# Moving the per-chunk products of a delta-rule layer out of its recurrence, into items of one tile

## Chip, cores and metric
One core of a Trainium2 chip. The metric is the device time of one execution in microseconds (us); "before" is the median of three runs. Shorter is better.

## What is computed
Token ids (8 x 512) pick rows of an 8000 x 256 table; an attention layer of 16 heads of 16 channels (a delta rule with a running average, in chunks) is added to them, then a feed-forward layer with a router (top 2 of 8 experts and one shared expert, 256 -> 512 -> 256). All is float32. The kernel uses chunks of 32 tokens, 16 per batch. The heart of the reference, for one chunk i with keys K, queries Q, values V and B = beta * K:

```
T = tril(B @ K.T, -1);  inv = inverse(eye + T)
U = inv @ (V - B @ W_t)
W_new = W_t + K.T @ U
O = Q @ W_avg * a + Q @ W_t * c + T_mat * (Q @ K.T) @ U
W_avg_new = coef1 * W_avg + coef2 * W_t + K.T @ (U * w)
```

With Y = inv B and Z = inv V the update is U = Z - Y W, so that Y and Z need no state. Only W and W_avg go from chunk to chunk.

## The kernel before
It has three blocks that follow one another, each with one program per engine, in an order written out by hand; the engines meet at semaphores.

**First stage**, a loop over the 8 batches (512 tokens, 4 tiles of 128). GpSimd gathers the rows (`embed`), VectorE normalises them, TensorE turns them (`turn_x`, L378) and projects them to k, q, v in six 512-column groups (`project`, L399), the betas between the second and third (`beta`, L387). ScalarE copies each projection out twice (L490, L493), VectorE adds the three convolution taps (L577). Norms of k and q follow (`norms`, `spread_norms`, L408, L426, VectorE L609 to L625), the masks on ScalarE (L516, L521), and the Gram matrices and scores in two halves (`gram`, L452), taken by VectorE as ng (L642) and sT (L647). SP stores k, beta k and v, ng, scores and q to DRAM and loads the Gram matrices back, one chunk and pair of heads per partition (nx). The inverse is solved on VectorE by 62 half steps per batch (`half_step`, L172 and L175, both inputs in SBUF), dealt out between the other VectorE operations of the next two batches. Batches 0 to 5 are solved here, with the first 44 half steps of batch 6.
GpSimd also gathers the residual stream h in lane order (32 gathers) and adds the output bias to its 32 tiles (L366) while batches 0 to 2 run.

**Second stage**, the recurrence: 32 steps, two groups of 16. A step takes one chunk of four batches ("lanes"). TensorE applies the inverse to beta k and v (`yz`, 16 matmuls, L811, against a block-diagonal inverse), ScalarE copies that out twice (L938, L939), TensorE picks Z (`take_z`, 16 matmuls, L821), adds Y times the state (`read_y`, L833), ScalarE copies u (L945). Then `grow` (L859) sums K^T U, VectorE masks the new state (L1025), `read_q` (L847) reads the state by the queries, scaled on GpSimd (L789, four at a time), and `inside` adds scores times U (64 matmuls, L870). The output is normalised per head, turned, projected (`project`, L887), added to h (L1052), normalised and routed. VectorE does the rest of the inverses of batches 6 and 7 in steps 0 to 9, eight half steps per step. SP loads the inputs of step s+2 when the buffers of step s are free, in one queue.

**Third stage**: the shared expert on all batches, then 71 slots of 128 rows through the experts; TensorE is in it from 904 us on (L1229, L1235, L1264, L1271, L1286).

A matmul of float32 appears as two records in the profile, a transpose as one.

## Time and profile before

| what | value |
|---|---|
| runs, us | 1505.49, 1498.99, 1519.77; median 1505.49 |
| profiled execution, us | 1498.91, span 1497.1 |
| granted clock of TensorE, mean | 0.849 of full |
| busy: TensorE, VectorE, ScalarE, GpSimd | 1164.3, 749.3, 452.9, 321.9 us |

Engines in the rows: PE is TensorE, PEld its weight loads, DVE VectorE, ACT ScalarE, POOL GpSimd, SP the queue that issues DMAs. A row of a timeline has start, duration, engine, line, operation, output and inputs, and in brackets how long the engine was idle before it and what released it. "issue" means that the profile shows nothing that it waited for. In rows of busy times the order of engines is PE, PEld, DVE, ACT, POOL, each with its number of instructions.

### The profile page before, as it was taken

The page shows a single profiled execution, that of the slowest core. Times are in us where ns is not written, and L with a number is a line of the kernel's source. Part 1 is how long each engine was busy: PE and PEld are TensorE (multiplying, and loading weights), DVE is VectorE, ACT ScalarE, POOL GpSimd, SP SyncE. Part 2 cuts the span into 40 slices and gives each one's busy share as a digit, 9 for nine tenths or more (in the row PEclk, how much of TensorE's full clock was granted, in tenths as well). Part 3 has the DMA queues.
Part 4 walks back from the last instruction along what each step waited for, and adds up shares of the span by engine and source line. Part 5 has one row for each costly group of instructions (what it writes and reads, how often), then busy time and mean ns, then how long its engine had stood idle before and what let it go on. Part 6 is the DMA issues. An engine that isn't in the chain of part 4 may idle for free. (4 is left out here: it accounts for less than half of the span.)

```text
span 1497.1 us, 35306 instructions
## 1 busy us (share of the span) xinstructions
PE 1164.3 (78%) x14558; PEld 796.8 (53%) x14558; DVE 749.3 (50%) x1707; ACT 452.9 (30%) x889; POOL 321.9 (22%) x309
## 2 busy tenths in 40 slices
PE   4843765665655067778887878999999999999997
PEld 2632434434444056666676764665566666666664
DVE  4689999899999436754444453112111121211111
ACT  3540534424435022222332323331122222222221
POOL 3686101000000011110011104661022222222222
PEclk9875777778778557687888878999999999999999
DMA  7642555464556676567665619952132222223222
GB/s 272 189 145 63 147 153 116 132 162 103 143 111 158 160 158 152 130 143 165 157 148 141 160 56 342 346 167 78 28 47 47 46 47 44 46 47 47 47 46 29
DMA packets 232444, 184.00 MB, mean 123 GB/s; under 512 B 148165, under 2 KB 196197, under 8 KB 227937
## 3 DMA queue, kind: packets, MB, share of 16 engines
q1 hardware_dynamic: 198000, 149.20, 38.0%
q0 software_dynamic: 16368, 19.96, 7.6%
q10 hardware_dynamic: 17920, 12.59, 3.1%
q8 instruction: 119, 1.95, 0.5%
q14 instruction: 37, 0.30, 0.1%
HBM read 101.69 MB, written 86.26 MB: 126 GB/s over the span
## 5 line engine op out<-in xcount | busy, mean ns | idle before, releaser
L1420 DVE TENSOR_TENSOR hid_all<-p_s,silu 128x512 f32<-128x512 f32 x103 | 71.3, 692 | 378.5 <-PE p_s L1271 249.7
L1470 POOL DMA_INDIRECT out_h<-y_sb,x_in x71 | 110.8, 1560 | 360.7 <-DVE y_sb L1432 342.8
L1328 ACT ACTIVATE silu<-p_m 128x512 f32<-128x512 f32 x103 | 61.5, 597 | 328.2 <-PE p_m L1264 223.4
L175 DVE TENSOR_TENSOR xt<-xt,prod 128x62 f32<-128x62 f32 (+15 forms) x248 | 151.8, 612 | 4.3
L1286 PE MATMUL p_y<-wo,hid_all 128*128 x568 | 134.4, 380 | 0.8 <-ACT hid_all L1345 0.8
L1264 PE MATMUL p_m<-wi,xT_c 128*128 x284 | 133.6, 593 | 0.5 <-ACT xT_c L1341 0.5
L1271 PE MATMUL p_s<-ws,xT_c 128*128 x284 | 133.6, 593 | 0.0
L172 DVE TENSOR_TENSOR prod<-nx,xt 128x62 f32<-128x62 f32 (+15 forms) x248 | 129.6, 523 | 2.6
L577 DVE SCALAR_TENSOR_TENSOR cv<-raw,conv_sb,cv 128x512 f32<-128x512 f32 x144 | 107.0, 747 | 18.0 <-ACT raw L493 17.2
L1286 PEld LDWEIGHTS p_y<-wo,hid_all 128*128 128x128 f32 x568 | 102.5, 190 | 12.3 <-issue 1.4
L452 PE MATMUL p_g<-kqM,kT 32*32 32x128 f32 x2048 | 50.7, 369 | 71.2 <-DVE sT L647 53.8
L399 PE MATMUL p_p<-xT,wqkv_sb 128*128 128x512 f32 x192 | 105.2, 706 | 0.7 <-ACT xT L487 0.7
L490 ACT ACTIVATE cv<-p_p,now_b,conv_sb 128x512 f32<-128x512 f32 x48 | 37.3, 777 | 198.8 <-PE p_p L399 198.8
L789 POOL TENSOR_TENSOR qq<-qq,cst_early 128x512 f32<-128x512 f32 x32 | 33.8, 1089 | 286.4 <-DMA qq<-q_channels_dram 286.4
L452 PEld LDWEIGHTS p_g<-kqM,kT 32*32 32x32 f32 x2048 | 43.3, 133 | 76.7 <-issue 74.0
L870 PE MATMUL p_o<-u,sT_b 32*32 32x16 f32 x4096 | 52.6, 191 | 37.7 <-issue 37.6
L811 PE MATMUL p_yz<-xbd,bv_b 128*32 128x128 f32 x1024 | 43.2, 316 | 43.6 <-DMA xbd<-chunk_inverse_dram 34.5
L1264 PEld LDWEIGHTS p_m<-wi,xT_c 128*128 128x128 f32 x284 | 53.9, 190 | 38.3 <-issue 34.7
L1432 DVE COPY y_sb<-p_y 128x256 f32<-128x256 f32 x71 | 30.2, 425 | 85.5 <-PE p_y L1286 85.5
L1460 POOL DMA_INDIRECT slots_in_dram<-rows,slot_of x64 | 62.1, 971 | 45.8 <-ACT rows L1336 32.3
L870 PEld LDWEIGHTS p_o<-u,sT_b 32*32 32x32 f32 x4096 | 47.0, 121 | 45.5 <-issue 45.3
L399 PEld LDWEIGHTS p_p<-xT,wqkv_sb 128*128 128x128 f32 x192 | 42.0, 232 | 53.8 <-issue 45.3
(139 smaller groups left out, 1938.0 us busy)
## 6 DMA issues: line engine op xcount, KB each, us to landing
slots_in_dram<-h SPq DMA_DIRECT2D x9, 1040.0 KB, 10.0
x_in<-slots_in_dram SPq DMA_DIRECT2D x71, 130.0 KB, 2.1
k_tokens_dram<-kk SPq DMA_DIRECT2D x32, 256.0 KB
chunk_gram_dram<-ng SPq DMA_DIRECT2D x32, 256.0 KB
beta_kv_dram<-bv SPq DMA_DIRECT2D x32, 256.0 KB
nx<-chunk_gram_dram SPq DMA_DIRECT2D x8, 1024.0 KB, 4.9
xt<-in_const SPq DMA_DIRECT2D x8, 1024.0 KB, 8.0
scores_dram<-sT SPq DMA_DIRECT2D x32, 256.0 KB
```

The source lines that it names most:

```text
L172: ins = dve.tensor_tensor(pr, nx[b % 2][:, m, :, 0:m].rearrange("p e k -> p k e").unsqueeze(3).to_broadcast([P, m, 2, w]), xt[b % 2][:, m, ...
L175: ins = dve.tensor_tensor(kept, kept, pr, ALU.add)
L399: ins = pe.matmul(p_p[n % 2][:], wqkv_sb[:, k, p, m * P:(m + 1) * P], xT[:, k, :], start=(k == 0), stop=(k == KH - 1))
L452: ins = pe.matmul(p_g[c * C:(c + 1) * C, g % 4, t % 2, g // 4, :], kT[r, g // 4, tok], kqM[r, g // 4, :, :, tok].rearrange("p w e i -> p ( ...
L577: ins = dve.scalar_tensor_tensor(cv[:, p, m, :], raw[:, p, m, j:j + L], conv_sb[:, p, m, j:j + 1], cv[:, p, m, :], ALU.mult, ALU.add)
L870: ins = pe.matmul(p_o[lane(b), hd * DH:(hd + 1) * DH], sT[s % 2][lane(b), hd, :], u[s % 2][lane(b), hd * DH:(hd + 1) * DH], start=(chunk(s ...
L1264: ins = pe.matmul(p_m[n % 2][:], xT[s % 2][:, k, :], wi[:, e, k, :], start=(k == 0), stop=(k == KH - 1))
L1271: ins = pe.matmul(p_s[n % 2][:], xT[s % 2][:, k, :], ws[:, e, k, :], start=(k == 0), stop=(k == KH - 1))
L1286: ins = pe.matmul(p_y[s % 2][:, 0, :], hidT[s % 2][:, f * P:(f + 1) * P], wo[:, e, f, :], start=(f == 0), stop=(f == FK - 1))
L1420: dve.tensor_tensor(dst, p_s[n % 2][:], silu[n % 2][:], ALU.mult).then_inc(S["hid_ready"], 1)
L1460: pool.indirect_dma_start(xs_dram, bass.IndirectOffsetOnAxis(slot_of[:, t, k:k + 1], 0), rows[q][:, k, :], None).then_inc(s_scat[q], 16)
L1470: pool.indirect_dma_start(token_rows, bass.IndirectOffsetOnAxis(x_in[s % X_IN][:, D:D + 1].bitcast(U32), 0), y_sb[s % 2][:], None, compute ...
```

## The change
The work of a chunk that needs no state leaves the steps. It is done in "items": one item is one tile (four chunks) of one batch, 32 in all. An item loads inverse, beta k and v, and scores in one transfer (`load_item`), and its queries twice; applies the inverse (`apply_inverse`, 64 matmuls) giving -Y and Z; turns Y (`turn_y`); applies the scores to both (`apply_scores`, 64 matmuls), giving the part of the output that needs no state and a correction of the queries; adds the correction to the scaled queries (`sum_queries`, one matmul of 512 columns and four of 128); and stores all three (`store_item`). GpSimd scales the queries of an item (`scale_item`). A step then adds Z and the inner output by one matmul each (`take_z`, `take_o`), and Y and the corrected queries read the state as before; `yz`, `inside` and their copies are gone.

Items 0 to 19 (batches 0 to 4) are made in the first stage, four per batch from batch 3 on; items 20 to 31 (batches 5 to 7) in steps 0 to 3, 5 to 8 and 12 to 15 of the second stage. The two transposing banks of PSUM of the first stage become the items' banks, and x and v are turned in the projections' banks. In the first stage kk, bv, ng and sT now lie in the space of h, so the lane gather and the bias of h move to GpSimd in the second stage, and the slots' zero block is half as large. SP's order, ScalarE's order and VectorE's order in a step change with it. The stores of the scores and of beta k and v are one and two transfers instead of four and four. The third stage is unchanged.

```diff
+        AHEAD = 3
+        ITEMS = B * TILES
+        IN_A = TILES * (B - AHEAD)
+        R = 3
+        item = [sb(tail, f"item{i}", [P, 3, H, C]) for i in range(R)]
...
+        def load_item(sp, r):
+            b, t, i = r // TILES, r % TILES, r % R
+            if r >= R:
+                sp.wait_ge(T["q_summed"], r - R + 1)
+            sp.wait_ge(s_xst, 16 * HP * (b + 1))
+            sp.wait_ge(s_st, STORES * (b + 1))
+            sp.dma_start(item[i][:].rearrange("p w h i -> p (w h i)"),
+                         solve_dram[b, t * P:(t + 1) * P].rearrange("p w x -> p (w x)")).then_inc(s_item[i], 16)
...
+        def store_item(sp, r):
+            b, t, i = r // TILES, r % TILES, r % 2
+            at = (b // GROUP, slice(t * CH, (t + 1) * CH), slice(None), b % GROUP)
+            sp.wait_ge(T["y_ready"], r + 1)
+            sp.dma_start(y_dram[at].rearrange("c p x -> p c x"), y_out[i][:].rearrange("p c n i -> p c (n i)")
+                         ).then_inc(s_y_st[i], 16)
+            sp.wait_ge(T["yz_ready"], r + 1)
+            sp.wait_ge(T["inner_ready"], r + 1)
+            for c in range(CH):
+                sp.dma_start(zo_dram[t * CH + c, b], yzo[i][tok(c), 1:3].rearrange("p w h d -> p (w h d)")
+                             ).then_inc(s_zo_st[i], 16)
+            sp.wait_ge(T["q_ready"], r + 1)
+            sp.dma_start(qy_dram[at].rearrange("c p x -> p c x"), qy_out[i][:].rearrange("p c n i -> p c (n i)")
...
+        def scale_item(pool, r):
+            t, i = r % TILES, r % R
+            pool.wait_ge(s_item_q[i], 32 * (r // R + 1))
+            pool.tensor_tensor(item_q[i][:], item_q[i][:],
+                               table("q_scale")[:, t * P:(t + 1) * P].unsqueeze(1).to_broadcast([P, HQ, P]),
+                               ALU.mult).then_inc(T["q_scaled"], 1)
...
+        def apply_inverse(pe, r, bank, alone):
+            i = r % R
+            pe.wait_ge(s_item[i], 16 * (r // R + 1))
+            if r:
+                pe.wait_ge(T["fix_ready"], r)
+                pe.wait_ge(T["inner_ready"], r)
+                if alone:
+                    pe.wait_ge(T["q_ready"], r)
+            bv_i = item[i][:, 1].rearrange("p h i -> p (h i)").rearrange("p (w h d) -> p w h d", w=2, d=DH)
+            for hd in range(H):
+                for c in range(CH):
+                    ins = pe.matmul(bank[tok(c), hd * C:(hd + 1) * C], item[i][tok(c), 0, hd, :], bv_i[tok(c), :, hd, :],
+                                    start=True, stop=True)
+            ins.then_inc(T["solved"], 1)
...
+        def turn_y(pe, r, bank, alone):
+            pe.wait_ge(T["yz_ready"], r + 1)
+            if r and not alone:
+                pe.wait_ge(T["q_ready"], r)
+            for n in range(HQ):
+                ins = pe.transpose(bank[0:4 * DH, n * P:(n + 1) * P],
+                                   yzo[r % 2][:, 0, 4 * n:4 * n + 4, :].rearrange("p h d -> p (h d)"), ident)
+            ins.then_inc(T["y_turned"], 1)
...
+        def apply_scores(pe, r, bank, alone):
+            i = r % R
...
+            for hd in range(H):
+                for c in range(CH):
+                    ins = pe.matmul(bank[tok(c), hd * C:(hd + 1) * C], item[i][tok(c), 2, hd, :], yzo[r % 2][tok(c), 0:2, hd, :],
+                                    start=True, stop=True)
+            ins.then_inc(T["scored"], 1)
...
+        def sum_queries(pe, r, bank, alone):
+            pe.wait_ge(T["y_ready"], r + 1)
+            pe.wait_ge(T["fix_ready"], r + 1)
...
+            pe.wait_ge(T["q_scaled"], r + 1)
+            pe.matmul(bank[:], ident, item_q[r % R][:].rearrange("p n l -> p (n l)"), start=True, stop=False, skip_group_check=True)
+            for n in range(HQ):
+                ins = pe.matmul(bank[0:4 * DH, n * P:(n + 1) * P], q_fix[r % 2][:, n, :], ident, start=False, stop=True,
+                                skip_group_check=True)
+            ins.then_inc(T["q_summed"], 1)
...
+        def yz_out(act, r, bank):
+            act.wait_ge(T["solved"], r + 1)
...
+                        i0 = TILES * (b - AHEAD)
+                        if b >= AHEAD:
+                            load_item(sp, i0 + 2)
+                            if i0:
+                                store_item(sp, i0 - 1)
+                            load_item(sp, i0 + 3)
+                            store_item(sp, i0)
...
+                        if b >= AHEAD:
+                            store_item(sp, i0 + 1)
+                        if b + 1 >= AHEAD:
+                            load_item(sp, i0 + TILES)
...
+                                if b >= AHEAD:
+                                    store_item(sp, i0 + 2)
+                                if b + 1 >= AHEAD:
+                                    load_item(sp, i0 + TILES + 1)
...
-                    for s in range(NT):
-                        if s == NT // 2:
-                            embed(RING + 1)
-                        pool.tensor_tensor(h[:, s, :], h[:, s, :], bout_sb[:], ALU.add)
...
+                    for b in range(AHEAD, B):
+                        if b + 2 < B:
+                            embed(b + 2)
+                        for t in range(TILES):
+                            scale_item(pool, TILES * (b - AHEAD) + t)
...
                     for b in range(B):
                         pe.wait_ge(s_xT, b * KH + KH)
                         project(b, 0)
                         project(b, 1)
+                        solve_item(b, 0)
+                        score_item(b, 0)
                         beta(b)
-                        for n in range(2, 6):
-                            project(b, n)
+                        project(b, 2)
+                        project(b, 3)
+                        end_item(b, 0)
+                        solve_item(b, 1)
+                        project(b, 4)
+                        project(b, 5)
                         norms(b)
                         turn_v(b)
+                        score_item(b, 1)
                         spread_norms(b)
                         turn_k(b)
+                        end_item(b, 1)
+                        solve_item(b, 2)
+                        score_item(b, 2)
                         gram(b, 0)
+                        end_item(b, 2)
+                        solve_item(b, 3)
                         if b + 1 < B:
                             turn_x(b + 1)
+                        score_item(b, 3)
                         gram(b, 1)
+                        end_item(b, 3)
...
+                        scored_item(b - 1, 3)
+                        ended_item(b - 1, 3)
...
+                            if n == 1:
+                                solved_item(b, 0)
+                                scored_item(b, 0)
+                            if n == 3:
+                                ended_item(b, 0)
+                                solved_item(b, 1)
...
+                        scored_item(b, 1)
...
+                        ended_item(b, 1)
+                        solved_item(b, 2)
...
+                        scored_item(b, 2)
+                        ended_item(b, 2)
+                        solved_item(b, 3)
...
+            step_of = {IN_A + k: k for k in range(4)}
+            step_of |= {IN_A + 4 + k: 5 + k for k in range(4)}
+            step_of |= {IN_A + 8 + k: 12 + k for k in range(4)}
+            item_in = {s: r for r, s in step_of.items()}
...
+                    def load_step(s):
...
                         if s >= 2:
...
+                        if c % CH == 0:
+                            sp.wait_ge(s_y_st[t % 2], 16 * done)
+                            sp.wait_ge(s_zo_st[t % 2], 16 * CH * done)
+                            sp.wait_ge(s_qy_st[t % 2], 16 * done)
+                        if c:
+                            sp.dma_start(yy[i][:].rearrange("p b n i -> p (b n i)"), y_dram[g, c].rearrange("p b x -> p (b x)")
...
+                        sp.dma_start(zo[i][:].rearrange("p w d -> p (w d)"),
+                                     zo_dram[c, b:b + GROUP].rearrange("b i x -> (b i) x")).then_inc(s_zo[i], 16)
...
                     for s in range(NT):
-                        if s == 6:
+                        load_step(s)
+                        if s == 3:
                             store_inverse(sp, B - 2)
-                        if s == 14:
+                        if s == 11:
                             store_inverse(sp, B - 1)
-                        if s == NC_BATCH:
...
+                        if s - 2 in item_in:
+                            store_item(sp, item_in[s - 2])
+                        if s + 1 in item_in and item_in[s + 1] >= IN_A + 2:
+                            load_item(sp, item_in[s + 1])
...
+                    pool.wait_ge(s_weights, 16 * 5)
...
+                    def add_bias(n):
+                        pool.wait_ge(s_lane[n % 4], 16 * (n // 4 + 1))
+                        pool.tensor_tensor(h[:, n, :], h[:, n, :], bout_sb[:], ALU.add).then_inc(s_hb, 1)
...
+                    scale_item(pool, IN_A)
+                    scale_item(pool, IN_A + 1)
+                    pool.memset(h[:, 4:], 0.0).then_inc(s_hz, 1)
+                    pool.wait_ge(s_hz, 2)
+                    for n in range(NT):
+                        add_bias(n)
+                        if n + 4 < NT:
+                            gather(n + 4)
+                        if n + 1 in item_in and item_in[n + 1] >= IN_A + 2:
+                            scale_item(pool, item_in[n + 1])
 
                 @block.tensor
...
+                        ins = pe.matmul(p_u, ident, zo[s % 2][:, 0], start=True, stop=(chunk(s) == 0), skip_group_check=True)
...
+                        ins = pe.matmul(p_o[:], ident, zo[s % 2][:, 1], start=True, stop=(chunk(s) == 0), skip_group_check=True)
...
                     for s in range(NT + 4):
+                        r = item_in.get(s)
+                        if s < NT:
+                            read_y(s)
                         if s >= 4:
                             route(s - 4)
+                        if r is not None:
+                            apply_inverse(pe, r, p_i, True)
                         if s < NT:
-                            read_y(s)
+                            grow(s)
+                            take_o(s)
                             read_q(s)
+                        if r is not None:
+                            turn_y(pe, r, p_i, True)
                         if 1 <= s <= NT:
                             turn_o(s - 1)
-                        if s < NT:
-                            grow(s)
-                            if s + 1 < NT:
-                                yz(s + 1)
-                            inside(s)
+                        if 2 <= s < NT + 2:
+                            turn_xn(s - 2)
+                        if r is not None:
+                            apply_scores(pe, r, p_i, True)
                         if 1 <= s <= NT:
                             project(s - 1)
                         if s + 1 < NT:
                             take_z(s + 1)
-                        if 2 <= s < NT + 2:
-                            turn_xn(s - 2)
+                        if r is not None:
+                            sum_queries(pe, r, p_i, True)
...
                     for s in range(NT + 2):
+                        r = item_in.get(s)
                         if s < NT:
                             u_out(s)
+                        if s >= 2:
+                            row_sqrt(s - 2)
+                        if r is not None:
+                            yz_out(act, r, p_i)
+                        if s < NT:
+                            square(s)
+                        if r is not None:
+                            turned_y_out(act, r, p_i)
                         if 1 <= s <= NT:
                             oT_out(s - 1)
-                        if s + 1 < NT:
-                            yz_out(s + 1)
+                        if s >= 2:
+                            xnT_out(s - 2)
+                        if r is not None:
+                            scored_out(act, r, p_i)
                         if s < NT:
-                            square(s)
                             head_sqrt(s)
-                        if 1 <= s <= NT:
-                            row_sqrt(s - 1)
+                        if r is not None:
+                            queries_out(act, r, p_i)
...
                     for s in range(NT + 4):
+                        if 2 <= s < NT + 2:
+                            norm(s - 2)
+                        solve(SHARE * s)
+                        if s >= 4:
+                            take_score(s - 4)
+                        if s < NT:
+                            state_out(s)
+                        solve(SHARE * s + 2)
+                        if s < NT:
+                            head_sum(s)
                         if s >= 4:
                             gate(s - 4)
-                        solve(SHARE * s)
-                        if s < NT:
-                            state_out(s)
-                            head_sum(s)
-                        solve(SHARE * s + 2)
-                        if 1 <= s <= NT:
-                            residual(s - 1)
                         solve(SHARE * s + 4)
                         if s < NT:
                             head_norm(s)
                         solve(SHARE * s + 6)
                         if 1 <= s <= NT:
-                            norm(s - 1)
+                            residual(s - 1)
```

## Rows read from the trace of the kernel before

**Rows 1.** Busy times by stretch; columns: stretch, length, busy us, clock, DMA share, GB/s.
```profile
63.00:124.00 61.00, 33.56 (x426) 24.37 (x417) 54.43 (x79) 24.46 (x40) 50.13 (x55) 0.75 0.53 141
...
249.00:309.00 60.00, 35.33 (x384) 25.15 (x384) 55.25 (x115) 24.58 (x40) 0.00 (x0) 0.76 0.53 133
...
689.00:879.00 190.00, 158.14 (x5350) 130.02 (x5342) 88.66 (x330) 59.23 (x146) 16.92 (x16) 0.82 0.63 146
...
904.00:1497.00 593.00, 581.94 (x2074) 354.32 (x2074) 113.93 (x197) 148.87 (x310) 179.69 (x167) 0.99 0.36 88
```
**Rows 2.** Timeline (start us, us, engine, line, operation): projections 2 to 5 of batches 1, 2, 6, 7.
```profile
68.84 7.11 PE L399 MATMUL p_p<-xT,wqkv_sb 128*128 128x512 f32 x16
...
149.66 9.99 PE L399 MATMUL p_p<-xT,wqkv_sb 128*128 128x512 f32 x16
...
389.45 9.56 PE L399 MATMUL p_p<-xT,wqkv_sb 128*128 128x512 f32 x16
...
449.21 8.70 PE L399 MATMUL p_p<-xT,wqkv_sb 128*128 128x512 f32 x16
```
**Rows 3.** Timeline: betas of batches 0 and 6; Gram halves after batch 6's projections.
```profile
26.35 1.86 PE L387 MATMUL p_g<-wbeta_sb,xT 128*128 128x16 f32 x16
...
386.04 3.57 PE L387 MATMUL p_g<-wbeta_sb,xT 128*128 128x16 f32 x16 [8.42 <-DVE sT L647]
...
420.31 2.20 PE L452 MATMUL p_g<-kqM,kT 32*32 32x128 f32 x128 [1.83 <-ACT kqM L521]
...
425.88 0.68 DVE L642 TENSOR_TENSOR ng<-p_g,neta 128x512 f32<-128x512 f32 x1
...
430.22 3.53 PE L452 MATMUL p_g<-kqM,kT 32*32 32x128 f32 x128 [6.69 <-DVE sT L647]
```
**Rows 4.** Timeline of batch 1: a half step and the bias adds.
```profile
103.60 11.74 DVE L175 TENSOR_TENSOR xt<-xt,prod 128x462 f32<-128x462 f32 x1
103.93 10.91 POOL L366 TENSOR_TENSOR h<-h,bout_sb 128x256 f32<-128x256 f32 x16
```
**Rows 5.** Timeline of ScalarE: u of steps 1, 15, 16 and 31.
```profile
543.62 0.37 ACT L945 COPY u<-p_u 128x256 f32<-128x256 f32 x1 [0.54 <-PE p_u L833]
...
713.23 0.37 ACT L945 COPY u<-p_u 128x256 f32<-128x256 f32 x1 [0.28 <-PE p_u L833]
...
720.97 0.37 ACT L945 COPY u<-p_u 128x256 f32<-128x256 f32 x1 [0.28 <-ACT xnT L983]
...
878.91 0.37 ACT L945 COPY u<-p_u 128x256 f32<-128x256 f32 x1 [1.30 <-PE p_u L833]
```
**Rows 6.** Timeline of TensorE: the second part of one score group.
```profile
707.57 1.07 PE L870 MATMUL p_o<-u,sT_b 32*32 32x16 f32 x101 [2.98 <-issue]
```
**Rows 7.** The page's third part, DMA queues: packets, MB, share.
```profile
q8 instruction: 119, 1.95, 0.5%
```
**Rows 8.** Timeline: GpSimd's multiplies and VectorE operations beside them.
```profile
563.12 4.23 POOL L789 TENSOR_TENSOR qq<-qq,cst_early 128x512 f32<-128x512 f32 x4 [24.45 <-DMA qq<-q_channels_dram]
...
566.56 0.88 DVE L172 TENSOR_TENSOR prod<-nx,xt 128x62 f32<-128x62 f32 x1
...
707.74 4.23 POOL L789 TENSOR_TENSOR qq<-qq,cst_early 128x512 f32<-128x512 f32 x4 [42.78 <-DMA qq<-q_channels_dram]
...
710.68 0.42 DVE L1052 TENSOR_TENSOR h<-p_turn,h 128x256 f32<-128x256 f32 x1 [1.17 <-PE p_turn L887]
```
**Rows 9.** Timeline of TensorE: groups at the upper clock, first and second stage.
```profile
422.44 1.09 PE L378 MATMUL p_t<-cst,xhat 128*128 128x128 f32 x8
...
713.88 1.08 PE L811 MATMUL p_yz<-xbd,bv_b 128*32 128x128 f32 x32
...
715.89 1.18 PE L870 MATMUL p_o<-u,sT_b 32*32 32x16 f32 x118 [0.70 <-issue]
...
719.27 0.64 PE L821 MATMUL p_u<-cst_early,yz_ch 128*32 128x64 f32 x27 [0.91 <-issue]
```
**Rows 10.** Chain that ended last, last stage: start us, us, engine, tile, line.
```profile
934.67 1.72 PE p_m L1229 x4
```

389 lines of the change are left out of this document (198 added, 191 removed).

## Prediction

> **What bounds the kernel now.** I read the busy times by stretch first, then the timeline of each engine around the seams. The kernel has three stages. The last, from 904 us on, is TensorE at 98% busy under a full clock [rows 1]; no line of the change touches it, so its 593 us stand [rows 1]. All that can move lies in the first 904 us.
> In the first stage one batch takes 59.8 us (389.45 to 449.21) [rows 2], and VectorE is the bound: in a batch-long window it is busy 55.25 of 60 us, while TensorE has 35.33, ScalarE 24.58, at a mean granted clock of 0.76 [rows 1]. TensorE waits for VectorE twice per batch, 8.42 us before the betas and 6.69 us before the second half of the Gram matrices [rows 3]. One batch is longer: from 68.84 to 149.66 is 80.8 us [rows 2]. There a half step of the inverse, normally 0.6 us, stands in VectorE for 11.74 us, exactly while GpSimd adds the output bias to 16 tiles of h in 10.91 us [rows 4]; the same pair comes once more at 121 us.
> In the second stage (recurrence, 32 steps) TensorE is the bound: 158.14 of 190 us busy at a clock of 0.82 [rows 1]. From step 1 to step 31 the copies of u stand 335.3 us apart, 11.2 us a step; the best step is 7.74 us (713.23 to 720.97) [rows 5]. The difference between 7.7 and 10.5 (the mean after step 13) has two sources. One is the clock. The other is holes in the middle of the score group, 2.98 us in the row, released by nothing the profile shows [rows 6]; they come about once per step, and the instruction queue fetches 119 blocks over the whole span [rows 7].
>
> **Part 1: bias and lane gather leave the first stage.** The two VectorE stalls go: 11.74 and 11.75 less the 0.65 that such a step takes, -22 us, of which I take -21.5 (80.8 against 59.3 for the batches around it). Nothing else was waiting in that batch that would take its place: TensorE there waited for the same VectorE results. In the second stage the bias adds (32 of them, 0.68 us each) and the gathers sit on GpSimd again; VectorE has two-SBUF-input work there only in the half steps of steps 0 to 9, so they cost at most some 5 us of VectorE time, inside steps that TensorE bounds. I take 0, bounds 0 to +6. Why PSUM matters: the residual add h<-p_turn,h ran in 0.42 us, its normal time, in the middle of a GpSimd run of four multiplies [rows 8].
>
> **Part 2: the query scaling joins the first stage.** 20 of the 32 items are scaled there by GpSimd, in one 128x512 multiply each; four of them took 4.23 us, 1.06 each [rows 8]. A half step that met such a run was held until its end (0.88 instead of 0.22 us) [rows 8]. Four items per batch, VectorE nearly all on such half steps and taps: up to 4 x 1.06 = 4.2 us per batch; an item whose multiply meets a PSUM operation or an idle moment costs nothing. I take 3.0, bounds 1 and 4.2.
>
> **Part 3: item work on TensorE and ScalarE in the first stage.** An item is two groups of 64 32x32 matmuls, 4 transposes, one 512-column matmul and four of 128 columns. At full clock: a score group of 118 records took 1.18 us, so 128 take 1.28; 8 transposes took 1.09, so 4 take 0.55; four records of 512 columns took 1.72, so two take 0.86, and four of 128 columns the same again [rows 9, 10]. Sum 2 x 1.28 + 0.55 + 0.86 + 0.86 = 4.8 us. At the low clock the betas took 3.57 instead of 1.86 [rows 3]; the item is then 8 to 9 us. Four items add 19 to 35 us to TensorE's 35 in a 60 us batch. ScalarE gets five copies per item, some 2.5 us, 10 per batch on 24.6: it has room.
> What decides is the place. Items 0 and 3 stand in the two waits of 8.42 and 6.69 us. There they are covered, and they keep TensorE busy through what is now idle time after which the clock is low. The end of item 0 and the solve of item 1 stand between projections 3 and 4, and the projections feed VectorE's taps with about 1 us to spare; at full clock they add 3.0 us, against which the betas give back up to 1.7 and the projections 2.4 (16 records took 9.56 us) if the clock has stayed up [rows 2, 3]. Then comes the scoring of item 1 before the norms are spread, covered by statistics and reciprocal on VectorE. Last, the end of item 1 and item 2 up to its scores stand before Gram half 0, whose second mask on ScalarE now also waits behind the copies of items 1 and 2: that group ended at 422.5, VectorE takes it at 425.88 [rows 3], 3.4 us of cover against some 4 to 6 us. The later half has 8 us of cover. I take +1.2 us per batch net for all of this, bounds 0 and +6. The added loads and stores (nine DMAs per item on SP's queue, some 18 us of issue per batch beside 20 now, and about 0.3 to 0.4 of DMA share beside 0.53 [rows 1]) stand in SP's queue before the stores of k and the load of the Gram matrices; that load has some 15 us before VectorE wants it. I take 0 and keep +4 per batch in the slow rival.
> First stage: -21.5 + 5 x (3.0 + 1.2) = -0.5 us; bounds -21.5 + 5 x 1 = -16 and -21.5 + 5 x 14 = +49.
>
> **Part 4: the recurrence.** Each step loses the Y/Z group (1.08), the scores group (1.28) and the picking of Z (27 records 0.64, so 32 take 0.76): 3.1 us at full clock. It gains two one-matmul additions of 256 columns, 0.43 each [rows 9, 10]. The best step of 7.7 becomes 5.5. A chain shows up under it: square, head sum, gate, root, normalisation, residual on VectorE and ScalarE, which I add up to 6.2 us from their own durations. The real mean is now 1.36 times the best (10.5 over 7.74) [rows 5]; with the same factor a plain step is 7.5, an item step (5.5 + 4.8) x 1.36 = 14.0 us. VectorE has 6 us of its own per step and 4.4 of half steps in steps 0 to 9, so the two plain steps there stay at the 11.2 of now. One more wait: the load of item 28 stands on SP behind the store of the last inverse (8 DMAs, 7.1 us of issue, then the landing), and the loads of step 12 stand behind it, so step 11 takes 13. Steps 1 to 30: 11 x 14.0 + 2 x 11.2 + 7.5 + 13 + 15 x 7.5 = 309.4 against 335.3 [rows 5]: -26. Bounds: item steps 11.5 to 12.5, plain 6.6: about -60; item steps at the low clock 16.5, plain 9: +30.
> Where the trace shows holes inside a group of matmuls, the Trainium skill (Runtime: NRT & Kernel Launch, Instruction fetch mechanics) says that instructions come in blocks of 256 by the sequencer's own DMA queue and that crossing a block costs mostly nothing. The 2.98 us row disagrees. By that page the holes would be nothing here and the item steps would be some 1.5 us cheaper, which would add about 18 us to the gain; the rows decide for me.
> The entry of the stage loses the wide loads (block-diagonal inverse, queries) and GpSimd's zeroing of xbd: -2. The exit gets one step more of latency (the normalisation of step 31 is one pass later): +1.
>
> **Sum.** The profiled execution took 1498.9 us (span 1497.1). -0.5 - 26 - 2 + 1 = -27.5 gives 1471. The median of the runs is 1505.5, 0.44% above, so 1478.
>
> **Rivals.**
> A. *Item work in the first stage is hidden and the low-clock stretches go.* GpSimd's multiplies mostly meet nothing (5 us in all), TensorE stays at the upper level, item steps near 12 and plain steps near 6.6. For: waits of 8.42 and 6.69 us, rows at both clock levels. Against: the half step held to the end. -16 - 55 - 1 = -72 at the far end, some -62: 1444.
> B. *TensorE becomes the bound of the first stage (slower).* Item groups are almost only tiny matmuls, the kind that shows the holes; with low clock and two blocks per item an item costs 8.6 + 1.5 = 10 us, four of them 40 on 35, with 4 us of serial waits (norms, roots) 79 us for a batch of 60. It decides from 64 us on, where it eats the 21.5 gained. Price: 5 x 19 = +95, less 21.5, less 27: +46, so 1552. For: a mean clock of 0.76. Against: the busier TensorE is, the higher the clock in these rows (0.99 in the last stage) [rows 1].
> C. *The recurrence gains nothing.* The 12 item steps take back what the plain steps give (16 us each against 7.5): 0 from that stage, first stage about 0: 1503 to 1510.
>
> **Chances.** Forecast (1455 to 1495) 0.45, A 0.22, C 0.19, B 0.14. Two per cent, which is about what a measurement of this kernel tells from no change (the three runs span 1.4%), is 30 us; the faster line is 1475.4, just below my number. Faster: A 0.22, and 0.21 of the forecast. Same: 0.24 of the forecast, 0.16 of C. Slower: B 0.14 and 0.03 of C. Range: from within A to within B, 1438 to 1530; the forecast's own range is 1455 to 1495.
>
> **What would show it.** Right: the 11.7 us half steps gone, batch 1 near 60 us; batches 3 to 7 at 63 to 66 us with half steps of 1 to 1.6 us beside GpSimd multiplies; TensorE's waits at the betas and the second Gram half shrunk to 0 to 3; plain steps 7 to 8 us, steps 12 to 15 near 14; a late step 11 or 12. Wrong: batches over 70 us with VectorE waiting for raw or p_g (B), plain steps still near 10 (then the chain on VectorE or the loads bound them), or the stretch from 904 on of another length.

## The result, and the profile after

The kernel after the change takes 1521.85 us (median of 20 runs, 1514.06 to 1530.2) against 1506.13 before (20 runs, 1497.45 to 1519.77): 1.0106 times as long, 95% interval 1.0083 to 1.0129. It is slower by 1.1%, clear of the noise of 20 runs each but inside the 2% that the prediction counts as no change; 1478 was forecast. The two profiled executions differ by more, since the one of before was near its fastest run: spans 1522.6 and 1497.1, +25.5 us. The rest of this section splits those 25.5.

Busy times by stretch after the change (stretch, length, busy us per engine, clock, DMA share, GB/s), against [rows 1]:
```profile
334.00:406.00 72.00, 54.51 (x1468) 38.72 (x1467) 58.77 (x114) 33.09 (x60) 5.54 (x4) 0.90 0.64 192
740.00:900.00 160.00, 139.10 (x3154) 105.62 (x3154) 94.07 (x352) 45.31 (x137) 34.97 (x40) 0.90 0.64 192
930.00:1522.60 592.60, 581.58 (x2074) 353.65 (x2073) 112.88 (x194) 148.91 (x310) 179.45 (x167) 0.99 0.36 87
```
The last stage is what it was. In a batch with items VectorE is busy 58.8 us, 3.5 more than before, but idle 13.2 of 72 (before 4.8 of 60), and TensorE, busy 54.5 at a clock of 0.90, isn't full either. So each waits in turn for a result of the other.

Timeline of TensorE: projections after the betas, batches 1, 2, 6, 7, against [rows 2] (there 68.84, 149.66, 389.45, 449.21):
```profile
67.73 7.11 PE L531 MATMUL p_p<-xT,wqkv_sb 128*128 128x512 f32 x16
...
125.03 5.24 PE L531 MATMUL p_p<-xT,wqkv_sb 128*128 128x512 f32 x6
...
406.06 5.38 PE L531 MATMUL p_p<-xT,wqkv_sb 128*128 128x512 f32 x8
...
484.25 5.68 PE L531 MATMUL p_p<-xT,wqkv_sb 128*128 128x512 f32 x8
```
Batch 1 has shrunk from 80.8 to 57.3 us, batch 6 has grown from 59.8 to 78.2. Starts of the betas give the sum: those of batch 3 come at 182.13 instead of 205.38 (-23.3), and from there to the first u it is 388.6 us instead of 322.9 (+65.7, 13.1 per batch). The first u stands at 570.76 instead of 528.28: +42.5.

Timeline of batch 6, ScalarE, VectorE and TensorE (in brackets: idle before, and what ended it):
```profile
421.09 0.59 ACT L294 COPY yzo<-p_item 128x512 f32<-128x512 f32 x1 [7.16 <-DMA z_and_inner_dram<-yzo]
...
422.96 0.75 DVE L769 SCALAR_TENSOR_TENSOR cv<-raw,conv_sb,cv 128x512 f32<-128x512 f32 x1 [5.87 <-ACT raw L671]
...
426.39 4.24 PE L540 MATMUL p_g<-kqM,cst_early 128*32 128x128 f32 x32 [8.24 <-ACT kqM L683]
...
446.81 2.01 PE L585 MATMUL p_g<-kqM,kT 32*32 32x128 f32 x107
452.08 1.10 PE L585 MATMUL p_g<-kqM,kT 32*32 32x128 f32 x21 [3.26 <-issue]
...
453.31 0.69 DVE L838 TENSOR_TENSOR h<-p_g,neta 128x512 f32<-128x512 f32 x1 [4.90 <-PE p_g L585]
```
Two things are to be seen. ScalarE's copy of Y and Z waits 7.16 us for a store of the item two before; the copies of projections 4 and 5 stand behind it, so VectorE waits for raw and TensorE 8.24 us for the squares. And the first Gram half, which stands behind the item groups, stops for 3.26 us in its middle with no releaser; VectorE then waits 4.90 us. Such a stop inside a group of matmuls, with nothing that the profile shows as waited for ("issue"), is called a hole below. The waits from 185 to 560 us, by line:
```profile
DVE cv L769 <- ACT raw L671: 35.0, 12, 5.9
...
PE p_g L585 <- issue: 21.6, 10, 3.3
DVE h L838 <- PE p_g L585: 20.8, 5, 5.5
PE p_item L273 <- issue: 20.2, 13, 3.6
ACT yzo L294 <- DMA z_and_inner_dram<-yzo: 19.6, 4, 7.2
```
(us in total, times, longest.) The holes of TensorE in this stretch, those of L253 included, add up to some 45 us, 9 per batch; before there are none from the betas of batch 3 on. The instruction queue fetches 140 blocks, of 16 KB each, instead of 119 [rows 7]:
```profile
q8 instruction: 140, 2.29, 0.6%
```
Recurrence: u of steps 1, 12, 13, 30 and 31 on ScalarE, against [rows 5], and the score group in the middle of step 2:
```profile
590.76 0.37 ACT L1123 COPY u<-p_u_turn_x 128x256 f32<-128x256 f32 x1 [0.45 <-PE p_u_turn_x L1019]
...
755.48 0.37 ACT L1123 COPY u<-p_u_turn_x 128x256 f32<-128x256 f32 x1 [9.35 <-PE p_u_turn_x L1019]
773.03 0.37 ACT L1123 COPY u<-p_u_turn_x 128x256 f32<-128x256 f32 x1 [0.45 <-PE p_u_turn_x L1019]
...
899.65 0.37 ACT L1123 COPY u<-p_u_turn_x 128x256 f32<-128x256 f32 x1 [1.78 <-PE p_u_turn_x L1019]
905.46 0.37 ACT L1123 COPY u<-p_u_turn_x 128x256 f32<-128x256 f32 x1 [1.78 <-PE p_u_turn_x L1019]
```
```profile
619.34 0.53 PE L273 MATMUL p_item<-yzo,item 32*32 32x32 f32 x20 [3.07 <-issue]
```
A plain step is 5.8 us, an item step mostly 17 to 20 (step 5 24.3, step 15 10.2), and in steps 1 and 2 the score group stops for 3.07 us at the same place, after 107 and 108 records. From step 0 to 31 it is 334.7 us instead of 350.6 (-15.9; from step 1, 314.7 instead of 335.3). From u of step 31 to the end: 617.1 instead of 618.2. +42.5 - 15.9 - 1.1 = 25.5.

What the holes wait for is in the same trace, in the packets of the instruction queue. From 20 to 910 us TensorE has 45 holes of over 0.5 us; 44 of them end 1.2 to 1.6 us after a packet of that queue has landed (before: all 29 of such holes). Each step with an item sees three such packets, only step 15 two; each plain step sees one, step 19 none.

### The profile page after: what moved, and what is told of

It is laid out like the page before. It is cut to its first block and busy times, and to the rows that moved or that the text cites. A ratio compares the mean times of both kernels' runs of the same rounds, so it can differ in the third digit from the quotient of the medians.

```text
span 1522.6 us, 40964 instructions
## 1 busy us (share of the span) xinstructions
PE 1246.2 (82%) x17182; PEld 836.7 (55%) x17182; DVE 742.0 (49%) x1707; ACT 478.9 (31%) x985; POOL 324.2 (21%) x308
## 5 line engine op out<-in xcount | busy, mean ns | idle before, releaser
L238 POOL TENSOR_TENSOR item_q<-item_q,cst_early 128x512 f32<-128x512 f32 x32 | 40.8, 1276 | 513.7 <-DMA item_q<-q_channels_dram 513.7
L769 DVE SCALAR_TENSOR_TENSOR cv<-raw,conv_sb,cv 128x512 f32<-128x512 f32 x144 | 115.9, 809 | 47.0 <-ACT raw L671 46.1
L174 DVE TENSOR_TENSOR xt<-xt,prod 128x62 f32<-128x62 f32 (+15 forms) x248 | 133.1, 536 | 4.4
L273 PE MATMUL p_item<-yzo,item 32*32 32x32 f32 x4096 | 51.2, 198 | 59.8 <-issue 55.6
L585 PE MATMUL p_g<-kqM,kT 32*32 32x128 f32 x2048 | 48.1, 327 | 42.7 <-issue 21.6
L273 PEld LDWEIGHTS p_item<-yzo,item 32*32 32x32 f32 x4096 | 44.2, 109 | 66.6 <-issue 66.1
L1652 POOL DMA_INDIRECT slots_in_dram<-rows,slot_of x64 | 62.1, 971 | 46.4 <-ACT rows L1528 33.1
L1624 DVE COPY y_sb<-p_y 128x256 f32<-128x256 f32 x71 | 30.1, 424 | 85.5 <-PE p_y L1478 85.5
L1463 PEld LDWEIGHTS p_s<-ws,xT_c 128*128 128x128 f32 x284 | 48.5, 191 | 34.4 <-issue 34.4
L1421 PE MATMUL p_m<-xnT_c,wi 128*128 128x512 f32 x128 | 62.0, 608 | 5.3 <-DMA wo<-in_w_out 5.3
```

The source lines that it names most:

```text
L174: ins = dve.tensor_tensor(kept, kept, pr, ALU.add)
L273: ins = pe.matmul(bank[tok(c), hd * C:(hd + 1) * C], item[i][tok(c), 2, hd, :], yzo[r % 2][tok(c), 0:2, hd, :], start=True, stop=True)
L769: ins = dve.scalar_tensor_tensor(cv[:, p, m, :], raw[:, p, m, j:j + L], conv_sb[:, p, m, j:j + 1], cv[:, p, m, :], ALU.mult, ALU.add)
L1421: ins = pe.matmul(p_m[n % 2][:], wi[:, SHARED, k, cols], xnT[b % 2][:, k, :], start=(k == 0), stop=(k == KH - 1))
L1463: ins = pe.matmul(p_s[n % 2][:], xT[s % 2][:, k, :], ws[:, e, k, :], start=(k == 0), stop=(k == KH - 1))
L1652: pool.indirect_dma_start(xs_dram, bass.IndirectOffsetOnAxis(slot_of[:, t, k:k + 1], 0), rows[q][:, k, :], None).then_inc(s_scat[q], 16)
```

## The experiments

Times are medians; a ratio is to the kernel before, run on the same chip in the same rounds. "First stage" is the time of the first u, "recurrence" the time from u of step 0 to u of step 31, both in the profiled execution. After the change they were 570.8 and 334.7.

**1. GpSimd's scaling left out of the first stage.**
```diff
-                        for t in range(TILES):
-                            scale_item(pool, TILES * (b - AHEAD) + t)
```


> Leaves out GpSimd's scaling of the queries of items 0 to 19 (20 multiplies of 1.09 us beside VectorE, so the rows of these queries are unscaled); all else as after the change. Theory lock (my prediction's part 2): VectorE, which bounds a batch, loses 3 us per batch to these multiplies, so five batches get 15 us shorter (5 to 21) and VectorE's busy time in batches 3 to 7 falls from about 58 to 55 us. Theory order (the batches are long because TensorE and ScalarE, which run their orders as written, bring projections, copies and Gram groups late): VectorE's busy time falls the same way, but its waits grow by as much; the total changes by 0 to -5 us and a batch stays at 72 to 77 us.


1517.85 us, 1.0079 [1.0048, 1.0110], 2 to 6 us less than after. VectorE's busy time from the betas of batch 3 to the first u falls from 291.3 to 279.2 us, 2.4 per batch, but its waits grow: for the betas from 7.2 to 11.7 us, for the norms from 1.3 to 7.5. Theory order holds: the time that the multiplies cost is real in VectorE's busy time, and worth about 1 us of a batch at the end.

**2. One matmul in place of each group of 64, first stage.** Values of Y, Z and scores product of items 0 to 19 aren't the real ones.
```diff
+            if not alone:
+                ins = pe.matmul(bank[:], ident, item[i][:, 0]..., start=True, stop=True)
-            for hd in range(H):
+            for hd in range(H if alone else 0):
```


> In the items of the first stage (0 to 19) the two groups of 64 matmuls of 32x32 are replaced by one 512-column matmul each, so Y, Z and the scores product of these items are not the real ones; waits, copies, DMAs and the places in the orders stay. Theory size (the groups cost TensorE what they last: 2 x 1.3 to 2.6 us plus the holes of 1 to 3.6 us seen in them, and what follows waits for it): some 5 to 8 us per batch go, total -25 to -40 us, TensorE's busy time per batch falls from 57 to about 47 us, and waits named issue in the middle of groups nearly vanish from the first stage. Theory order (each item is a chain of five hand-overs between TensorE and ScalarE standing in front of what VectorE wants, whatever the matmuls last): -5 to -15 us. Theory transfers (a batch is long because item transfers and their place in SP's queue hold ScalarE): 0 to -5.


1465.72 us, 0.9744 [0.9693, 0.9796], 56 less than after: more than any theory gave. Only 23 us of it lie in the first stage (548.0). The recurrence, whose own groups are untouched, went from 334.7 to 296.9. The stage part supports size. The rest raised the question of runs 5 and 6: the edit takes 20 x 126 matmuls of four instructions out ahead of the recurrence, 10080, which is 39 blocks of 256 and 96 more, so the blocks of the recurrence end elsewhere as well (100 blocks are fetched instead of 140).

**3. A third buffer for Y, Z and inner outputs.**
```diff
-yzo = [... for i in range(2)]
+yzo = [... for i in range(3)]
...
-            if r >= 2:
-                act.wait_ge(s_zo_st[r % 2], 16 * CH * (r // 2))
+            if r >= 3:
+                act.wait_ge(s_zo_st[r % 3], 16 * CH * (r // 3))
```


> Three buffers for Y, Z and the inner outputs instead of two, so ScalarE's copy of Y and Z no longer waits for the store of the item two before. Theory transfers: the waits of 6.3, 3.6, 7.2 and 2.6 us in batches 4 to 7 go, and since five projections' worth of taps stand behind them, -15 to -20 us in total (a batch of 71 to 72 instead of 75). Theory order or size: VectorE finds its next late result within the same batch (the Gram group, the norms), so at most -8 us.


1510.96 us, 1.0039 [1.0009, 1.0069], 11 less than after. The wait for the store is gone from ScalarE's list, VectorE's for raw falls from 35.0 to 23.0 us. First stage 558.9 in this profile (569.9 in run 15, whose first stage is the same code: single profiles differ by this much, 570.8 and 574.6 for the changed kernel itself). The total, not this difference, is what shows the gain: the two ratios to before, 1.0039 and 1.0106, have intervals that don't meet. It lies between the two theories (15 to 20, at most 8). A cause, but the smaller one.

**4. The scoring of item 2 behind the first Gram half.**
```diff
-                        score_item(b, 2)
                         gram(b, 0)
+                        score_item(b, 2)
```


> On TensorE the scoring of item 2 stands behind the first half of the Gram group instead of in front of it. Theory order: VectorE's wait for the first Gram half (3.0 to 5.5 us per batch, 20.8 us in all) goes, and TensorE's scoring falls into the time between the halves, where TensorE waits for VectorE: -10 to -20 us. Theory size or transfers: the group comes earlier but the later steps (end of item 2, solve of item 3, transposes of x, second half) come later by as much: 0 to -5 us.


1526.06 us, 1.0129 [1.0078, 1.0179]: nothing gained. VectorE's waits for Gram halves are 24.3 us, now ten times instead of five, and the first half waits for ScalarE's masks of q, which stand behind the item copies (16.2 us in five).

**5. Moved block ends.** Extra tiny matmuls at the start of TensorE's program.
```diff
+                    for _ in range(16):      # 32 and 48 in the other two
+                        pe.matmul(p_i[0][0:32, 0:32], ident[0:32, 0:32], ident[0:32, 0:32], start=True, stop=True)
                     turn_x(0)
```


> 16 extra 32x32 matmuls (64 instructions: each is two weight loads and two matmuls) at the very start of TensorE's program, before anything waits for it; all else as after the change. They shift where the blocks of the fetched instruction stream end. Theory fetch: the holes named issue stand where a block ends inside a dense run of tiny matmuls, and an item step of the recurrence is 772 instructions by my count, close to 3 x 256, so the holes stand at the same place in each item step; with another shift they fall elsewhere: steps 0 to 31 of the recurrence, 334.7 us, change by more than 8 us in at least one of the three shifts (297 to 345), and the first stage (571 us) by more than 5 us. Theory data: the recurrence of the run with one matmul per group was short (297 us) because its data were other ones; then all three shifts give 333 to 338 us there and 568 to 573 us before it.

> As the run before, with 32 extra matmuls (128 instructions). Theory fetch: half a block away from where the change stands now, the hole of 3.07 us leaves the middle of the score group; recurrence 300 to 325 us. Theory data: 333 to 338 us.

> As the run before, with 48 extra matmuls (192 instructions). Theory fetch: different from the other two shifts and from none by more than 8 us in the recurrence. Theory data: 333 to 338 us.


1533.89, 1534.95 and 1527.16 us, ratios 0.9891, 0.9894 and 0.9857, on a chip where the kernel before took 1549.7; the changed kernel wasn't run on it, so the ratios say nothing of the shift. Recurrences: 328.6, 331.5 and 307.0 us. The holes in them add up to 40, 42 and 30 us, against 50 in the changed kernel. First stages: 591.9, 587.9 and 600.6 us, which can't be told from what made before slow there. The third shift speaks for theory fetch, whose figure for half a block (300 to 325) failed; with no unshifted run beside them the three don't show it, runs 11 and 15 do.

**6. The same shift in the kernel before.**


> The kernel before the change with 32 extra 32x32 matmuls at the start of TensorE's program. Its steps are not a multiple of 256 instructions, so its 20 holes at L870 already fall at every place: theory fetch gives 1500 to 1512 us (within 0.5% of before), with the long and the short steps of the recurrence in other places of the list. If instead its time moves by more than 1%, the comparison of the two kernels itself hangs on where the blocks end.


1552.5 against 1549.7 us, 1.0011 [0.9981, 1.0041]: no difference, as the ratio was expected; the 1500 to 1512 us were not met, because this chip took 1549.7 without the shift too.

**7. The changed kernel again**, on a chip like the first.


> The changed kernel itself, on the same chip as the next three, because the chip of the shift runs ran the kernel before at 1550 us instead of 1505. Ratio to before 0.985 to 1.012, whichever chip it is; on a chip like the first, recurrence 333 to 338 us, first stage 568 to 575.


1522.79 us, 1.0123 [1.0075, 1.0172]; first stage 574.6, recurrence 333.4.

**8. Item steps spread over the recurrence.**
```diff
+            step_of = {IN_A + k: s for k, s in enumerate((0, 1, 3, 4, 6, 7, 9, 10, 13, 17, 21, 25))}
...
+                        if 1 <= s < 3:
+                            pe.wait_ge(S["h_ready"], s)
```


> The 12 item steps of the recurrence are spread: steps 0, 1, 3, 4, 6, 7, 9, 10, 13, 17, 21, 25 instead of 0 to 3, 5 to 8, 12 to 15 (one wait is added in steps 1 and 2 to keep a bank free of collisions). Same instructions otherwise. Theory fetch: three blocks per item step cannot be fetched in the step, but a plain step uses less than one, so a plain step between lets the queue catch up: item steps of 12 to 14 us instead of 17 to 18, plain ones 5.8 to 7, recurrence 275 to 310 us. Theory chain (an item step is long because the hand-overs of an item between TensorE and ScalarE stand in line with those of the step): 17 us wherever the item stands, recurrence 330 to 338.


1535.76 us, 1.0234 [1.0187, 1.0280]; recurrence 337.4, in a profile that is the fastest of the four runs (1521.72), so the median's 13 us over run 7 aren't in it. Item steps still take 16.5 to 23.7 us early on and 13.7 to 15.5 late, with longer neighbours (8.2, 9.4 and 7.6 us before the last three). The late ones are shorter than the 17 of theory chain, but the recurrence as a whole is no shorter: a plain step between does not let the queue catch up, and that part of theory fetch is refuted.

**9. Runs 2 and 3 together.**


> Both at once: three buffers for Y, Z and inner outputs, and one 512-column matmul in place of each group of 64 in the items of the first stage (their values are not the real ones). Alone they gave 12 and 23 us of the first stage, while with one matmul the waits for the store grew from 19.6 to 37.8 us. Theory: size and transfers are the two causes and nothing else of weight is left, so a batch is 60 to 64 us and the first stage 520 to 535 us long (as long as before, 528). Rival: the hand-overs in front of the projections and the Gram group cost by themselves, a batch stays above 66 us, first stage over 545.


1441.01 us, 0.9582 [0.9539, 0.9625]. First stage 515.7; batches 3 to 6 by the betas' starts 62.1, 62.2, 63.5, 59.7 us:
```profile
244.00:307.00 63.00, 49.64 (x459) 31.60 (x460) 59.69 (x117) 33.11 (x60) 10.33 (x9) 0.89 0.81 240
```
VectorE is nearly full again. The two causes together are 55 us of the first stage, alone 23 and some 10: with short groups the store wait had grown from 19.6 to 37.8 us, with a third buffer the groups still were late. Of the 65.7 us that the stretch from the betas of batch 3 to the first u had gained, 10.4 are left (333.3 against 322.9, 2.1 per batch), with the same transfers (DMA share 0.81), the same copies and the same places.

**10. Dense run, one place of the array.** 512 matmuls of 32x32 at two starts.


> Two runs of 512 extra 32x32 matmuls (2048 instructions, 8 blocks of 256), one at the start of TensorE's program, one at the start of its part of the recurrence; nothing else uses TensorE there. At the 20 ns per matmul of the trace they last 10.2 us each (20 at the low clock). Theory fetch: such a run is bound by the fetching of blocks, with a hole of 2.5 to 3.5 us about every 64 matmuls: 30 to 40 us each. Theory that blocks are read ahead and cost nothing: 10 to 21 us each, and the holes in the item groups have another cause.


One run, 1616.08 us. Timeline of TensorE, the two runs of 512:
```profile
11.43 54.82 PE L607 MATMUL p_item<-cst 32*32 32x32 f32 x1024 [11.43 <-DMA bbeta_sb<-in_bbeta]
...
609.09 54.82 PE L1092 MATMUL p_item<-cst 32*32 32x32 f32 x1024 [21.06 <-DMA ids_lane_sb<-in_ids_lane]
```
54.82 us at a granted clock of 1.00 and 54.82 at 0.50, 107 ns each, without one hole. Here every matmul uses the same place of the array, and 64 of them last 6.9 us, so the run doesn't test what dense groups like the items' do. It does show that blocks can come without a hole when each lasts 6.9 us: 8 instruction packets were fetched during the first run. Its recurrence took 332.1 us, though 512 matmuls, eight whole blocks, stand ahead of it twice.

**11. Third buffer and 192 instructions at the start.**


> Third buffer for Y, Z and inner outputs and the 192 instructions of shift, together, full computation. If where the blocks end is what made that run's recurrence 307 us on the slow chip: 12 us from the buffer and some 20 to 28 from the recurrence, 1480 to 1492 us. If the shift's gain was chance of that one profile: 1508 to 1514 us.


1487.62 us, 0.9886 [0.9838, 0.9934]; first stage 571.0, recurrence 302.4. Before took 1501.51 us here, and the record numbers the chip as that of runs 5 and 6.

**12. Dense run as the items have it**, four row groups in turn.
```diff
+                    for k in range(512):
+                        pe.matmul(p_i[tok(k % 4), k // 4 % 16 * 32:...], ident[tok(k % 4), 0:32], ident[tok(k % 4), 32:64], start=True, stop=True)
```


> As the dense run, but consecutive matmuls use the four row groups of the array and sixteen places of the bank in turn, like the item groups. Theory fetch: 20 ns each inside a block, and a hole of 3 to 5 us after each 64, so 4.5 to 6 us per block and 36 to 48 us per run of 512. Theory that the holes belong to the hand-overs of the item (semaphores, operands) and not to the instruction stream: no holes, 10 to 20 us per run.


One run, 1578.78 us. Timeline of TensorE in the first of the two:
```profile
11.45 3.68 PE L607 MATMUL p_item<-cst 32*32 32x32 f32 x223 [11.45 <-DMA bbeta_sb<-in_bbeta]
15.77 2.14 PE L607 MATMUL p_item<-cst 32*32 32x32 f32 x128 [0.64 <-issue]
19.50 1.99 PE L607 MATMUL p_item<-cst 32*32 32x32 f32 x128 [1.59 <-issue]
23.79 2.17 PE L607 MATMUL p_item<-cst 32*32 32x32 f32 x128 [2.29 <-issue]
27.80 1.93 PE L607 MATMUL p_item<-cst 32*32 32x32 f32 x128 [1.84 <-issue]
32.91 1.93 PE L607 MATMUL p_item<-cst 32*32 32x32 f32 x128 [3.18 <-issue]
```
After the first 223 records a hole after every 128, that is 64 matmuls or 256 instructions, with no operand to wait for and nothing else on the engine: 3.7 to 5.4 us from block to block here, 3.5 to 5.1 in the second run, 32.6 and 30.1 us per 512 instead of 10.2 at 20 ns each (36 to 48 were expected by theory fetch). The 1024 added matmuls add 16 blocks to the 140, so a block is 64 of them:
```profile
q8 instruction: 156, 2.56, 0.7%
```
The queue's packets in the trace close the argument. In the first of the two each hole ends 1.2 to 1.6 us after one has landed (those that end at 19.50, 23.79 and 27.80 us after landings at 17.91, 22.42 and 26.63), and a packet takes 0.9 to 1.2 us. From 15.77 us on it starts only 1.0 to 3.2 us after the block before it has begun to run; these three times make up the 3.7 to 5.4 us. The holes belong to the instruction stream. The clock doesn't enter: between the holes a block runs in 1.93 to 2.17 us at a granted 1.00 and in 1.93 to 2.20 us at 0.50. The recurrence took 333.4 us behind its eight whole blocks.

**13. One matmul per group in the recurrence's items** (values of items 20 to 31 aren't the real ones).


> In the items of the recurrence (20 to 31) one 512-column matmul stands in place of each group of 64 (their Y, Z and scores product are not the real ones); the first stage is as after the change. Theory size with holes: an item step is 17.5 us because its three blocks of instructions bring holes and a low clock; with 252 x 2 instructions fewer it takes 9 to 11 us, recurrence 250 to 270 us. Theory chain of hand-overs: 14 to 16 us, recurrence 300 to 320.


1450.00 us, 0.9655 [0.9607, 0.9703]; recurrence 259.2, item steps 8.7 to 15.5 us, half of them under 10, clock 0.92 there instead of 0.84, 116 blocks fetched instead of 140:
```profile
571.00:830.00 259.00, 234.77 (x3539) 164.95 (x3538) 185.71 (x595) 84.77 (x242) 72.16 (x73) 0.92 0.73 218
```
75 us for 24 blocks, 6.3 us per item, 3.1 per block. Theory size with holes. The holes in the recurrence fall from 50 to 6 us, 44 of the 75; the rest is the groups' own time and the lower clock, not told apart here.

**14. All of items 1 and 2 behind the first Gram half**, on ScalarE and SP too, with the third buffer.
```diff
-                        end_item(b, 1)
-                        solve_item(b, 2)
-                        score_item(b, 2)
                         gram(b, 0)
+                        end_item(b, 1)
+                        solve_item(b, 2)
+                        score_item(b, 2)
```


> Third buffer, and on TensorE the end of item 1, solve and scoring of item 2 all stand behind the first Gram half; on ScalarE their copies stand behind the masks of q and the copies of k, and SP's store of item 1 and load of the next batch's first item follow them. Full computation. Theory place: VectorE's wait for the first Gram half (21.6 us over five batches with three buffers) goes, first stage 558.9 to 540 us or below, total 1488 to 1500. Theory size: the same item work then delays the second half and the transposes of x, first stage 555 to 562, total 1506 to 1514.


1549.31 us, 1.0302 [1.0242, 1.0362], first stage 601.0: worse than both theories. In batch 5 VectorE no longer waits for the first half, but 5.17 us for the second, with a hole in it:
```profile
407.33 3.20 PE L586 MATMUL p_g<-kqM,kT 32*32 32x128 f32 x108 [3.88 <-issue]
...
410.56 0.69 DVE L839 TENSOR_TENSOR h<-p_g,neta 128x512 f32<-128x512 f32 x1 [5.17 <-PE p_g L586]
```
Waits for Gram halves rise from 21.6 to 41.1 us. The place was no third cause: the wait moved to the other half and grew.

**15. Third buffer, 192 instructions moved in the recurrence alone.** The 48 matmuls stand before `take_z(0)`.


> Third buffer, and the 192 instructions (48 tiny matmuls) now stand at the start of TensorE's part of the recurrence, where it waits 20 us for a load anyway; full computation, the first stage's stream is that of the run with three buffers. Theory fetch (the recurrence's length hangs on where its blocks end): first stage 559 to 563 us, recurrence 298 to 310, total 1475 to 1484. Theory that the shorter recurrence of e11 came from something else at the start: 335 us there, total 1508 to 1514.


1482.08 us, 0.9814 [0.9773, 0.9855]; first stage 569.9, recurrence 294.7, clock 0.88, holes 25 us. The u of step 31:
```profile
864.52 0.37 ACT L1128 COPY u<-p_u_turn_x 128x256 f32<-128x256 f32 x1 [1.78 <-PE p_u_turn_x L1022]
```
In the recurrence nothing but the block ends differs from run 3, whose last u is at 897.02 and whose recurrence is 338.1 us: 43 us less. The medians differ by less, 29 us (ratios 0.9814 and 1.0039, 2.3% or 34 us); this profile's first stage is 11 us longer than run 3's with the same code, and single profiles vary by as much. That TensorE has worked just before isn't the reason: in run 11 the matmuls stand 550 us earlier. Nor is it extra work as such: in eight profiles whose recurrence starts at the changed kernel's own place in a block (it, runs 1, 3, 4, 7 and 14, and runs 10 and 12 with whole blocks ahead) the recurrence takes 329.5 to 338.1 us.

**16. As 15, end of item 0 and solve of item 1 behind projection 5.**
```diff
-                        end_item(b, 0)
-                        solve_item(b, 1)
                         project(b, 4)
                         project(b, 5)
+                        end_item(b, 0)
+                        solve_item(b, 1)
```


> As the run before, and the end of item 0 and the solve of item 1 stand behind projection 5 instead of between projections 3 and 4, on TensorE and on ScalarE. Theory place: VectorE's waits for raw (23.0 us in five batches with three buffers) fall to 10 or less, total 5 to 12 us below the run before. Theory size: the norms and what follows come late by as much, 0 to +5.


1477.42 us, 0.9768 [0.9728, 0.9808]: the fastest version with the full computation, 1.9 to 2.7% faster than before. VectorE's waits for raw fall from 25.6 (12 times) to 19.5 us (5 times), not to the 10 of theory place. The step from 15 is 4.7 us, just under its 5 to 12, with overlapping intervals: likely, not shown.

## Why the prediction was wrong, by its steps

**The step that failed** is part 3's "I take +1.2 us per batch net for all of this", with part 2 4.2 a batch; measured 13.1. Of these, the dense groups and the store of Z together are 11 by run 9. Under it lies the price of a group: "a score group of 118 records took 1.18 us, so 128 take 1.28". That row [rows 9] is a stretch between two holes. An item is 512 instructions in its two groups, two blocks of 256, and a block takes 3.5 to 5.4 us to come when the run is dense (run 12): near 8 us per item on TensorE alone (an estimate, twice 4), not 2.6. The hole of 2.98 us was in the rows [rows 6] and the prediction took the rows against the page, but then put the holes in the slow rival only. By that page (the Trainium skill, Runtime: NRT & Kernel Launch, Instruction fetch mechanics: crossing a block mostly costs nothing) the gain would have been larger still. The trace agrees with it in plain steps, 232 instructions by my count in 5.8 us without a hole, and disagrees where 256 are used up faster than the next come: 2 us of work against 3.5 to 5.4 in run 12.

**"I take 0"** for the DMAs on SP's queue failed in another place than the one I kept +4 for: not the stores of k or the Gram load, but the store of Z. In batch 6 its values were ready at 388.0, SP issued it from 408.23 to 411.15, behind the wait for the Gram stores, the load of nx and an item's loads; ScalarE's next item copy waited for its landing until 421.09, and the projections' copies stood behind that. So 20 us went in SP's order and some 10 in the landing, which for such a store is otherwise 3.0 us (median); why this one was slow is not shown. Third buffer: 11 us of the total.

**The cover before the first Gram half** (3.4 us against 4 to 6) was read rightly and then priced at nearly nothing; VectorE waited 4.2 us per batch there. Moving the work (runs 4, 14) didn't help.

**Part 1** held: batch 1 is 57.3 us, -23.5 where -21.5 was taken; by the trace only, no run undid it alone. **Part 2** held in VectorE's time (2.4 us per batch, 3.0 taken), but little of it reaches the end of a batch that waits elsewhere (run 1). With short groups and the third buffer, a kernel that leaves work out, the first stage is 515.7, 12.6 us less than before where -0.5 was forecast. That its total (1441.01) is rival A's 1444 is chance: 45 us of it come from a recurrence of 305.5 us whose blocks end elsewhere.

**Part 4** came out near its sum (-20.6 for -26, step 1 to 31) by two errors that cancel. A plain step is 5.8 us, not 7.5, and those of steps 4 and 9 are 6.1 and 7.0, not 11.2: without the score group the late ones have no holes and run at a granted clock of 1.00. The factor of 1.36 was no property of a step; it had been made of holes (31 us in the steps from 13 on, 1.7 of the 2.8 us between mean and best) and of a clock of 0.82. An item step is 17.7 in the mean of the eleven, not 14.0: the factor was too small for two dense groups. Step 11 took 13.4 for 13. Without their groups item steps take 8.7 to 15.5 us, 11 in the mean (run 13).

**Rivals.** B had the right mechanism (holes, dense tiny matmuls, two blocks per item) and forecast batches of 79, which were 73 to 77 by the betas' starts; its bound was put wrongly, since TensorE wasn't full: VectorE and TensorE waited for each other by turns. Its counter-argument, that a busier TensorE gets a higher clock, was true (0.76 to 0.84-0.90) and not enough. C's total was nearest (1503 to 1510 for 1522) by luck, for another reason: the recurrence gained and the first stage lost.

**What hangs on chance.** With two dense groups an item step is 772 instructions by my count, close to 3 x 256, so a block ends near the same place of each such step, in the changed kernel inside the scores. The same recurrence took 295 to 307 us with 192 instructions ahead of it. The 1.1% of the result is thus this change with this placement; with a third buffer and the shift the same computation is 1.9% faster than before. What placement does to the first stage no run tells (run 11's 571.0 stands beside 558.9 and 569.9 in runs 3 and 15).

**Open:** why some placements make longer holes (the counts of holes differ less than their lengths), what sets the 1.0 to 3.2 us before a block's fetch starts, and how much of an item step is the hole and how much the low clock (0.78 granted up to step 12) beside it, since in the items the two always came together.

## What to carry to other kernels

Price dense runs of tiny matmuls by instructions, not by their records' durations: count 256-instruction blocks (64 float32 matmuls), and allow each 3.5 to 5.4 us; with 5.8 us and more of work per block, evenly spread, no hole was seen (plain steps, run 10). When work is moved into another engine's gaps, try one buffer more than the order seems to need, because the store that frees it stands in an in-order queue behind other waits (11 us of 1522 here). And before a change of 1 to 2% is believed, shift the instruction stream by a part of a block (192 instructions here) and time it again.

## Not expected of the hardware

Matmuls of 32x32 that all use the same place of the array took 107 ns each, at a granted clock of 1.00 as at 0.50; with four row groups in turn they took 30 to 34 ns inside a block (1.93 to 2.20 us per 64). In runs 5 and 6 the kernel before took 1549.7 us instead of 1505; in its profile with the shift the first Gram half of batch 0 kept VectorE waiting 46.5 us, with 31 holes of up to 2.6 us (33.4 in all) inside one group:
```profile
DVE ng L644 <- PE p_g L452: 46.5, 1, 46.5
...
PE p_g L452 <- issue: 33.4, 31, 2.6
```
From batch 0's betas to batch 1's it was 88.1 us instead of 40.8, of which batch 1 gave 15 back; the recurrence, 374.9 instead of 350.6 us, is another part. These holes aren't the block ends of above: they come mostly 1.4 us apart, with one or two matmul records between, and one 16 KB instruction packet was fetched in all that time. Nor were the DMA engines full (share 0.22 from 47 to 95 us). It isn't the chip alone either: the record numbers the chip of runs 11 to 14 the same, and there the kernel before took 1501.51 us. The cause stays open.
